# Attention scores of an AdaLN block: 32-row products by head group, in two visits of the tensor engine instead of four

## The reference, cut to what matters

```python
q = (h @ W_q).reshape(B, T, 16, 8);  k = (c_kv @ W_k_up).reshape(B, T, 16, 8)
scores = einsum('bqhd,bkhd->bhqk', q, k) + einsum('bqr,bkr->bqk', q_rope, k_rope)[:, None]
w = softmax(where(causal, -inf, scores / sqrt(8 + 32)))
x = x + (einsum('bhqk,bkhd->bqhd', w, v).reshape(B, T, 128) @ W_o)
y = sum_e cw[e] * (silu(c @ Wg[e]) * (c @ Wu[e])) @ Wd[e]   # 64 experts
x = x + y + shared_expert(c)
```

## Time and profile before

| | |
|---|---|
| median of 3 runs | 755.12 us (753.29 to 757.13) |
| the profiled execution's own time | 754.2 us |
| its span | 752.4 us |
| PE busy | 721.2 us, 96% of the span |
| DVE, ACT, POOL busy | 547.1, 453.3, 425.5 us |
| mean granted PE clock | 0.989 of 2.4 GHz |
| the opening, up to the first unit | 69.6 us |

### The profile page before, as it was taken

How to read it: one execution, slowest core, us unless ns; L and a number is a source line. 1 busy time by engine, 2 the same in 40 slices (tenths; PEclk the granted TensorE clock), 3 DMA queues, 4 the chain that set the end, 5 groups by cost and what they waited for, 6 DMA issues and landing times.

```text
span 752.4 us, 15834 instructions
## 1 busy us (share of the span) xinstructions
PE 721.2 (96%) x5644; PEld 556.2 (74%) x5644; DVE 547.1 (73%) x1150; ACT 453.3 (60%) x872; POOL 425.5 (57%) x349
## 2 busy tenths in 40 slices
PE   4788989999999999999999999999999999999997
PEld 3576767777787777777787777777777777877885
DVE  3867666886688856976778866888569766886664
ACT  2656875477555775567655775556755675555553
POOL 2456864555455655566455664566456555566665
PEclk8899999999999999999999999999999999999999
DMA  7494344434454364444545345443644344345451
GB/s 262 143 340 116 112 123 113 138 98 127 121 117 134 103 142 112 128 112 117 121 128 131 102 144 121 105 121 109 151 114 131 105 122 126 100 124 148 127 135 47
DMA packets 69055, 97.20 MB, mean 129 GB/s; under 512 B 8017, under 2 KB 26897, under 8 KB 68977
## 3 DMA queue, kind: packets, MB, share of 16 engines
q1 hardware_dynamic: 64512, 91.21, 44.8%
q10 hardware_dynamic: 4464, 4.98, 1.9%
HBM read 90.73 MB, written 4.98 MB: 127 GB/s over the span
## 4 chain that ended last, share of the span: by engine, by line
PE 75%; ACT 9%; DVE 8%; POOL 4%; issue 2%; DMA 1%; POOLq 0%; DVEq 0%; SPq 0%; ACTq 0%
PE Y L950 21%; PE U L950 20%; PE G L950 20%; PE A L950 12%; POOL hid_lo L613 2%; ACT s_t L378 2%; DVE act_w L921 2%; ACT hid_hi L517 2%; ACT L505 1%; DVE hid L933 1%; PE A L1011 1%; ACT L378 1%; ACT G L505 1%; DMA pooled_scratch<-hid 1%; DMA w<-in_weights 1%
## 5 line engine op out<-in xcount | busy, mean ns | idle before, releaser
L613 POOL TENSOR_TENSOR hid_lo<-hid,hid_hi 128x512 fp32r<-128x512 f32 (+1 forms) x264 | 342.2, 1296 | 277.5 <-ACT hid_hi L517 276.7
L921 DVE TENSOR_TENSOR act_w<-G,cwb 128x512 f32<-128x512 f32 x248 | 170.4, 687 | 99.8 <-ACT G L505 98.0
L505 ACT ACTIVATE G<-G 128x512 f32<-128x512 f32 x248 | 144.4, 582 | 149.3 <-PE G L950 147.5
L517 ACT CAST hid_hi<-hid 128x512 fp32r<-128x512 f32 (+1 forms) x264 | 162.3, 615 | 64.3 <-DVE hid L933 63.5
L933 DVE TENSOR_TENSOR hid<-act_w,U 128x512 f32<-128x512 f32 (+1 forms) x256 | 175.7, 686 | 23.4 <-PE Y L950 1.5
L950 PE MATMUL G<-c_hi,wg_hi 128*128 128x512 f32 x248 | 113.6, 458 | 0.0
L950 PE MATMUL Y<-hid_hi,wd_hi 128*128 128x512 f32 (+1 forms) x264 | 106.6, 404 | 5.3 <-POOL hid_lo L613 5.0
L950 PE MATMUL Y<-hid_hi,wd_lo 128*128 128x512 f32 (+1 forms) x264 | 103.5, 392 | 0.0
L950 PE MATMUL Y<-hid_lo,wd_hi 128*128 128x512 f32 (+1 forms) x264 | 103.5, 392 | 0.0
L950 PE MATMUL U<-c_hi,wu_hi 128*128 128x512 f32 x248 | 98.4, 397 | 0.0
L950 PE MATMUL G<-c_hi,wg_lo 128*128 128x512 f32 x248 | 97.7, 394 | 0.0
(11 more groups left out here) (183 smaller groups left out, 894.7 us busy)
## 6 DMA issues: line engine op xcount, KB each, us to landing
cwb<-cw_scratch SPq DMA_DIRECT2D x256, 256.0 KB, 3.7
k_blk<-in_cond_w SPq DMA_DIRECT2D x112, 64.0 KB, 2.3
wg_raw<-in_we_gate SPq DMA_DIRECT2D x8, 256.0 KB, 6.1
wu_raw<-in_we_up SPq DMA_DIRECT2D x8, 256.0 KB, 6.2
wd_raw<-in_we_down SPq DMA_DIRECT2D x8, 256.0 KB, 6.7
xf<-in_x_feat SPq DMA_DIRECT2D x8, 256.0 KB, 4.2
out_feat<-y ACTq DMA_DIRECT2D x8, 256.0 KB, 2.2
h_feat<-pooled_scratch SPq DMA_DIRECT2D x7, 256.0 KB, 2.7
```

The lines of the kernel that those rows point to most:

```text
L505: nc.scalar.activation(gate_bank(p)[:, :], gate_bank(p)[:, :], ACT.Silu).then_inc(S["silu_done"], 1)
L517: nc.scalar.copy(hid_hi[0:n, p % NH, :], hid[0:n, p % NH, :]).then_inc(S["hi_ready"], 1)
L613: nc.gpsimd.tensor_sub(hid_lo[0:n, p % NH, :], hid[0:n, p % NH, :], hid_hi[0:n, p % NH, :].bitcast(F32)).then_inc(S["lo_ready"], 1)
L921: nc.vector.tensor_mul(act_w[:, p % NH, :], gate_bank(p)[:, :], cwb[:, p % NCW, :])\
```

## The change

- ACT copies the queries once, whole, into `q_sb`; the other three copies and their masks are gone.
- A score product now contracts only the 32 rows of its head group (`q_sb[32g:32g+32]` with `k_blk[32g:32g+32]`), on the part of the array at row `32g` and column `32r`.
- The banks hold head groups instead of tiles: `A2` groups 0 and 2, `A1` groups 1 and 3, each with the scores of all 16 sequences for its 4 heads. `s_t` and `head_max` are laid out by group, and mask, maximum, subtraction and exponential go by group, with the same sizes.
- PE makes groups 0 and 1 in step 6 (32 products, alternating between the two groups) and groups 2 and 3 in step 8, and none in steps 7 and 9. Step 8 waits until DVE has reduced group 1 (`biased_tile` +2). Before, step 8 waited for the reduction of the first tile and step 9 for that of the second.
- The first transposes (step 12) wait for all four exponentials instead of the first, since each tile's rows now lie in all four groups.

```diff
-        s_t = sb("s_t", [P, TILES, HEADS * SEQ])
+        s_t = sb("s_t", [P, NG, TILES * HG * SEQ])
-        q_grp = sb("q_grp", [P, NG, TOK])
+        q_sb = sb("q_sb", [P, TOK])
@@ ACT, steps 1 to 4
                     if p == 1:
                         act.wait_ge(S["q_ps"], blk + 1)
-                    nc.scalar.mul(q_grp[:, p - 1, :], A2[:, :], C["group"][:, p - 1:p]).then_inc(S["q_ready"], 1)
+                        nc.scalar.copy(q_sb[:, :], A2[:, :]).then_inc(S["q_ready"], 1)
@@ DVE, steps 6 to 9
-                    s = s_t[:, t, :].rearrange("p (h k) -> p h k", k=SEQ)
-                    chain(nc.vector.tensor_add(s, (A2, A1)[t % 2][:, :].rearrange("p (h k) -> p h k", k=SEQ),
-                                               rope_mask[:, t, :].unsqueeze(1).to_broadcast([P, HEADS, SEQ])), blk)
+                    s = s_t[:, t, :].rearrange("p (t h k) -> p t h k", h=HG, k=SEQ)
+                    chain(nc.vector.tensor_add(s, (A2, A1)[t % 2][:, :].rearrange("p (t h k) -> p t h k", h=HG, k=SEQ),
+                                               rope_mask[:, :, :].unsqueeze(2).to_broadcast([P, TILES, HG, SEQ])), blk)
@@ PE
-                    pe.wait_ge(S["q_ready"], blk * NG + NG)
+                    pe.wait_ge(S["q_ready"], blk + 1)
...
-                elif 6 <= p < 10:
-                    t = p - 6
-                    if t == 0:
+                elif p in (6, 8):
+                    pair = (p - 6, p - 5)
+                    if p == 6:
                         pe.wait_ge(S["rope_mask_ready"], blk + 1)
                         pe.wait_ge(S["k_ready"], blk * HG + HG)
-                    elif t >= 2:
-                        pe.wait_ge(S["biased_tile"], blk * TILES + t - 1)
-                    for g in range(NG):
-                        for r in range(SPT):
-                            tok = bass.ts(t * SPT + r, SEQ)
-                            last = mm((A2, A1)[t % 2][32 * r:32 * r + 32, bass.ts(g, P)], q_grp[:, g, tok], k_blk[:, :, tok])
-                    last.then_inc(S["score_tile_ps"], 1)
+                    else:
+                        pe.wait_ge(S["biased_tile"], blk * NG + 2)
+                    for s in range(SPB):
+                        t, r = divmod(s, SPT)
+                        for g in pair:
+                            rows = slice(32 * g, 32 * g + 32)
+                            last = mm((A2, A1)[g % 2][32 * r:32 * r + 32, bass.ts(t, P)], q_sb[rows, bass.ts(s, SEQ)],
+                                      k_blk[rows, :, bass.ts(s, SEQ)], tile_position=(32 * g, 32 * r))
+                    last.then_inc(S["score_tile_ps"], 2)
                 if 12 <= p < 16:
                     t = p - 12
-                    pe.wait_ge(S["prob_tile"], blk * TILES + t + 1)
+                    pe.wait_ge(S["prob_tile"], blk * NG + NG)
...
-                        last = nc.tensor.transpose(A1[:, bass.ts(g, P)], s_t[:, t, bass.ts(g, P)], C["ident"])
+                        last = nc.tensor.transpose(A1[:, bass.ts(g, P)], s_t[:, g, bass.ts(t, P)], C["ident"])
```

More of the change, by code:

```diff
@@ L130, in adaln_attention_moe @@
         rope_mask = sb("rope_mask", [P, TILES, SEQ])
-        head_max = sb("head_max", [P, TILES, HEADS])
+        head_max = sb("head_max", [P, NG, TILES * HG])
         rden = sb("rden", [P, TILES, HEADS])
@@ L566, in attention_step @@
                     s = s_t[:, t, :].rearrange("p (h k) -> p h k", k=SEQ)
-                    nc.gpsimd.tensor_sub(s, s, head_max[:, t, :].unsqueeze(2).to_broadcast([P, HEADS, SEQ]))\
+                    nc.gpsimd.tensor_sub(s, s, head_max[:, t, :].unsqueeze(2).to_broadcast([P, TILES * HG, SEQ]))\
                         .then_inc(S["sub_tile"], 1)
@@ L672, in attention_step @@
                     dve.wait_ge(S["score_tile_ps"], blk * TILES + t + 1)
-                    s = s_t[:, t, :].rearrange("p (h k) -> p h k", k=SEQ)
-                    chain(nc.vector.tensor_add(s, (A2, A1)[t % 2][:, :].rearrange("p (h k) -> p h k", k=SEQ),
-                                               rope_mask[:, t, :].unsqueeze(1).to_broadcast([P, HEADS, SEQ])), blk)
-                    nc.vector.tensor_reduce(head_max[:, t, :], s, AX, ALU.max).then_inc(S["biased_tile"], 1)
+                    s = s_t[:, t, :].rearrange("p (t h k) -> p t h k", h=HG, k=SEQ)
+                    chain(nc.vector.tensor_add(s, (A2, A1)[t % 2][:, :].rearrange("p (t h k) -> p t h k", h=HG, k=SEQ),
+                                               rope_mask[:, :, :].unsqueeze(2).to_broadcast([P, TILES, HG, SEQ])), blk)
+                    nc.vector.tensor_reduce(head_max[:, t, :], s_t[:, t, :].rearrange("p (n k) -> p n k", k=SEQ), AX, ALU.max)\
+                        .then_inc(S["biased_tile"], 1)
                 elif 13 <= p < 17:
```

## The result

The changed kernel takes 749.06 us (median of 4 runs, 748.09 to 749.35), the kernel before 755.16 us (753.29 to 757.13) beside it. The ratio is 0.9917, with a 95% interval of 0.989 to 0.9943: faster by 6.1 us, where 9.7 was forecast (745.4 us). The sign held and the time lies inside the stated range (743 to 758 us), but the gain is 0.63 of the forecast one. The profiled execution took 748.1 us, its span is 746.3 against 752.4.

A forecast was written before the change was run, and what follows sets the result against it. PE, busy 96% of the span, was taken as the bound. Blocks 1 to 6 save 6 x 1.83 = 11.0 us, the opening loses 1.3: 9.7 less than 755.1, so 745.4 us; range 743 to 758 us.

The forecast's parts named there:

- The pace of the products: Score products on PE: two row groups run side by side, 13 ns a record instead of 26, bounded below by 9.
- rival 1: Score products: row groups don't overlap, pace stays 26 ns a record, 0.83 us more a visit, 757.1 us; chance 0.18.
- Rival 2: Score products: two row groups of one column obstruct each other, say 52 ns a record, +25 us, 779; chance 0.05.
- rival 3: Score products: half of the overlap, 18 to 22 ns a record, 750 to 753 us; chance 0.08.
- A visit still costs 1.2 us: Score visits on PE: 32 products cost what 16 did, so two visits fewer save 2.4 us a block.
- The wait gives back 0.57: Second visit (step 8): PE waits for DVE's reduction of group 1, leaving 1.83 of 2.4 us a block.
- The others follow: Blocks 1 to 6: ACT's run moves 1.83 us earlier, first transposes don't wait (0.25 us spare), fewer query copies worth nothing.
- rival 4: At the exponentials: POOL or DVE holds ACT's run, only 1.1 of 1.83 us arrives, 749.8 us; chance 0.09.
- The opening, +1.3: Before the first unit: group 2's products wait for group 1's reduction, letting DVE on 1.3 us later.
- theory B: Opening, for the missing 3.6 us: loses by the forecast wait and also by the clock, which falls because PE idles.
- Block 0, nothing: Block 0: gains nothing, since the chain there is a DMA landing, ACT and POOL.

The follow-up runs named there:

- e2: Changed kernel with four masked query copies and products over all 128 rows again, still two visits of 32: 759.84 us, ratio 1.0049 to the kernel before.
- e1: Changed kernel with all 16 products of one head group first in a visit, then the other's: 755.23 us, ratio 0.9982 to the kernel before.
- e5: Changed kernel with the second visit moved behind the gate of unit 4 in blocks with units: 745.87 us, ratio 0.9864 to the kernel before.
- e7: Kernel before, with its first transposes waiting for all four exponentials: 755.82 us, ratio 0.9997 to the kernel before.
- e6: Changed kernel with ACT copying the queries four times whole, each product reading its group's copy: 748.27 us, ratio 0.9887 to the kernel before.
- e3: Changed kernel with 13 more filler products on PE in the opening, behind the first and second visits: 747.62 us, ratio 0.9892 to the kernel before.
- e8: Changed kernel with e5's move, the opening's second visit split with a wait per group, and fillers before first visit and transposes: 742.76 us, ratio 0.9827.
- e12: e8 once more, same code, on the same chip as e11: 742.50 us, ratio 0.9803 to the kernel before.
- e9: The changed kernel once more, same code: 748.13 us (1 run).
- e10: e6 once more, same code: 750.12 us (1 run).
- e11: e8 with four whole copies of the queries in place of one: 741.15 us, ratio 0.9793 to the kernel before.

## Why the prediction was right and wrong

**The pace of the products: right.** 13 ns a record was taken between 9 and 26; 13.8 was measured. Rivals 1, 2 and 3 are out, and e2 shows what rival 1 would have cost in a block. Rival 1's premise, that products start strictly in order, does not fit e1 either, as its counts are read above. e1 adds that the order of the program decides how much the groups overlap. (Rival 2's time is 780 us by its own terms, not 779.) The Trainium skill (TensorE: Matmul & The Clock Gate, Part 1) has starts never closer than about 25 ns; the trace disagrees here too (13.8 ns). That pace would have taken the whole gain and not nearly all of it: an estimate from its figure and the prediction's 13 ns is 14 x 64 x 12 ns = 10.8 us. What the Trainium skill states in Part 3 of the same page, that tiles of different rows overlap, is borne out (a visit of 1.15 us against 2.02 in e2).

**A visit still costs 1.2 us: nearly.** By the same reckoning as in the prediction, the gate starts 255.45 - 254.04 = 1.41 behind the last up projection, 0.23 without a visit, and the second gate record 0.34 - 0.23 = 0.11 late: 1.29, where before it was 1.19. Two visits fewer are then 4 x 1.19 - 2 x 1.29 = 2.2 us, not 2.4.

**The wait gives back 0.57: right.** Without it the second visit would start 0.33 behind the up projection, at 260.24; it starts at 260.81. e5 measured 0.4 to 0.6 by removing it. Together 2.2 - 0.57 = 1.6 a block, measured 1.6 to 1.9, forecast 1.83. Six blocks gave 10.3 of the 11.0 us.

**The others follow: right.** ACT's run from silu to copy moved as one piece, the first transposes of block 2 do not wait, rival 4 is out. They do wait in the opening (1.10 us) and in block 0 (the other of the two waits above), but e7 shows that waiting for four exponentials costs nothing in blocks 1 to 6 or in the opening, and its block 0 keeps the 83.8 us of the others. The copies of the queries were worth nothing (e6).

**The opening, +1.3: this is the step that failed.** The term priced the wait of DVE, and that was right: 1.4 in e5. It put at nothing what a lower granted clock does there, where the chain runs through PE: the durations of PE were taken to stay what they were. The first unit came 3.3 us later; 2.0 us of the 3.6 that were missing are this. In the kernel after, 2.3 of the 3.3 have come by the mask of group 2 (33.72 - 27.55 = 6.17 against 3.86), 0.8 of it the visit at half speed (1.96 for 1.15), and 1.0 comes behind it, among the transposes. That the idle time which the change adds lowers the clock is not shown by itself: the clock falls before the new wait, in some executions of the code before as well (e7). In e3 it fell while PE was busy without a pause (from 26.75 us on), and it fell in e8, the same code as e12, with more work on PE in front of it (3.50 of 3.50 us and 3.27 of 4.10, in e12 2.62 and 3.27). Shown is what the low clock costs, that it was low somewhere in the opening in every trace of the kernel after (after, e9) and of its variants e1 to e6 and e10, and that it is at its upper level from 24 us on in e11 and e12, in both executions. Why it falls stays open, and the second half of theory B with it. The prediction had read durations of the opening from one execution in which the clock happened to be up.

**Block 0, nothing: off by 0.9**, by a landing that differs by up to 1.6 us over the fourteen traces (6.4 to 8.0) and by 1.3 between two of the same code (e6 6.7, e10 8.0). The prediction named that landing as what bounds block 0, but not as something that varies. The remaining 0.7 us stand in blocks 1 to 6. The visit that is 0.1 dearer accounts for them: 12 visits would be 1.2 by that reckoning, so it is rough.

Sum: 2.0 + 0.9 + 0.7 = 3.6, the distance between 9.7 and 6.1.

## What to carry to other kernels

Products that contract 32 rows take the least time on TensorE if neighbours in program order stand on different row groups (1.15 us a visit here, 1.56 group by group, 2.02 at full height); write the loop so that the groups alternate. Each group had its own bank here; whether that matters was not tested. When a change merges two waits into one later wait, put it behind work that needs nothing from it (here the next gate). Price the part of a kernel that isn't pipelined on its own, with its granted clock window by window, and from more than one execution: one microsecond of new waiting there (1.03 us) stood beside a low clock worth about 2.4.

## What the runs showed of the hardware

- Score products on eight tiles start eight records in a round of 109 ns, on four tiles four; the round is the same.
- By the count of starts in e1, TensorE takes products past a held-up neighbour, but only some 12 records ahead (the second group's first record after 20 of 32). The rows do not name the groups.
- The granted clock of the opening differs between executions of the same code: the first visit took 1.21 us in the kernel after, 1.48 in e9 and 1.15 in e5. The same code kept 1.00 from 24 us on in e12 and fell to 0.54 at 31.6 to 34 us in e8, with PE busier in front of it in e8. So what PE did just before does not settle it from these windows.
- The landing of the 256 KB store of `hid` took 6.7 us in one execution and 8.0 in another of the same code (e6, e10).
